# A graph layer kernel on one core: roots refined on GpSimd, half of the weights scaled on ScalarE, and another order of the front

## The reference

```python
h = relu(layernorm(x))                              # x: 2048 x 512, adj: 2048 x 2048, symmetric pattern
w_norm = (weight - mean(weight)) / std(weight, ddof=1)
wq  = round(clip(w_norm / wgt_alpha, -1, 1) * 7)    # weight: 512 x 512
xq  = round(min(h / act_alpha, 1) * 15)
support = relu((xq @ wq) * act_delta * wgt_delta)
sq  = round(min(support / act_alpha2, 1) * 15)
x   = x + ((adj / s) @ sq) * s * act_alpha2 / 15
h = relu(layernorm(x))
A = (adj + adj.T) / 2 + I;  d = rowsum(A) ** -0.5
x = x + adj @ ((d[:, None] * A * d[None, :]) @ h)
```

## Time and profile before

| | us |
|---|---|
| median of 3 runs (lowest, highest) | 508.2 (507.06, 508.78) |
| profiled execution | 508.43 |
| its span from first to last instruction | 506.5 |
| busy in it: PE | 489.6 (97%) |
| busy in it: DVE | 279.3 (55%) |
| busy in it: ACT | 141.3 (28%) |
| busy in it: POOL | 29.7 (6%) |

### The profile page before, as it was taken

The page is one execution under the profiler, slowest core; times in us unless marked ns, Lnnn a source line. Parts: engine busy times, 40 slices in busy tenths (PEclk is TensorE's granted clock), DMA queues, the critical chain, the costliest instruction groups (busy, mean ns, idle before and its releaser), DMA issues.

```text
span 506.5 us, 6411 instructions
## 1 busy us (share of the span) xinstructions
PE 489.6 (97%) x2404; PEld 238.8 (47%) x2404; DVE 279.3 (55%) x389; ACT 141.3 (28%) x198; POOL 29.7 (6%) x23
## 2 busy tenths in 40 slices
PE   2899999999899999999999999999999999999997
PEld 2646554554464444444444444444444444444443
DVE  5983989779979788787798777440010000100010
ACT  1576934425444143535431121240000000000000
POOL 0103710332000000000000000000000000000000
PEclk9999999999999999999999999999999999999999
DMA  8970676997944043232223322027001000000001
GB/s 295 402 299 1 177 155 164 212 257 167 291 139 146 0 128 122 83 118 89 83 84 124 122 85 83 0 79 274 21 22 41 21 21 21 34 28 21 21 21 41
DMA packets 39801, 56.86 MB, mean 112 GB/s; under 512 B 22888, under 2 KB 22888, under 8 KB 39784
## 3 DMA queue, kind: packets, MB, share of 16 engines
q1 hardware_dynamic: 39776, 56.63, 36.6%
q10 hardware_dynamic: 8, 0.00, 0.0%
HBM read 42.99 MB, written 8.39 MB: 101 GB/s over the span
## 4 chain that ended last, share of the span: by engine, by line
PE 90%; DVE 6%; DMA 2%; ACT 1%; issue 1%; ACTq 0%; POOL 0%; DVEq 0%; SPq 0%; POOLq 0%
PE ps_a L1020 33%; PE ps_p L919 18%; PE ps_p L983 7%; PE ps_a L983 7%; PE ps_b L983 7%; PE ps_m L983 4%; PE ps_h L983 4%; PE ps_a L901 2%; PE ps_b L901 2%; PE ps_b L873 1%; PE ps_m L919 1%; PE ps_h L919 1%; DVE st L552 1%; DVE small L774 1%; PE ps_a L873 1%; DMA a_in<-in_adj 1%
## 5 line engine op out<-in xcount | busy, mean ns | idle before, releaser
L919 PE MATMUL ps_p<-small,at 128*128 128x512 f16 x448 | 100.6, 379 | 0.0
L847 DVE SCALAR_TENSOR_TENSOR feat<-ps_a,feat 128x512 f32<-128x512 f32 x16 | 11.1, 691 | 153.8 <-PE ps_a L1020 153.8
L1020 PE MATMUL ps_a<-small,at 128*128 128x512 f16 x384 | 85.5, 379 | 0.0
L1020 PE MATMUL ps_a<-a_in,at 128*128 128x512 f16 x384 | 85.5, 379 | 0.0
L919 PEld LDWEIGHTS ps_p<-small,at 128*128 128x128 f16 x448 | 43.7, 98 | 47.9 <-DVE small L584 0.2
L457 ACT ACTIVATE split<-a_in 128x1024 f16<-128x1024 f32 x30 | 31.7, 1056 | 101.9 <-PE ps_p L983 90.0
L1020 PEld LDWEIGHTS ps_a<-a_in,at 128*128 (+1 forms) x384 | 37.6, 98 | 45.3
L1020 PEld LDWEIGHTS ps_a<-small,at 128*128 (+1 forms) x384 | 37.6, 98 | 45.3
L770 DVE TENSOR_TENSOR split<-a_in,split 128x1024 f16<-128x1024 f32 x30 | 36.7, 1224 | 34.0 <-ACT split L457 34.0
L983 PE MATMUL ps_p<-feat,split 128*128 (+1 forms) x180 | 43.9, 379 | 0.5 <-DVE small L774 0.5
L983 PE MATMUL ps_a<-feat,split 128*128 (+1 forms) x180 | 43.7, 379 | 0.0
(11 more groups left out here) (163 smaller groups left out, 422.6 us busy)
## 6 DMA issues: line engine op xcount, KB each, us to landing
a_in<-in_adj SPq DMA_DIRECT2D x54, 512.0 KB, 3.9
out<-feat SPq DMA_DIRECT2D x32, 256.0 KB, 2.4
feat<-in_x SPq DMA_DIRECT2D x8, 512.0 KB, 10.6
at<-in_adj SPq DMA_DIRECT2D x8, 512.0 KB, 14.2
feat<-out SPq DMA_DIRECT2D x4, 1024.0 KB, 9.5
at<-in_L_gnn_weight SPq DMA_DIRECT2D x2, 512.0 KB, 3.8
split<-in_adj SPq DMA_DIRECT2D x1, 512.0 KB, 16.5
tmp<-in_adj SPq DMA_DIRECT2D x1, 512.0 KB, 16.5
```

The lines of the kernel that those rows point to most:

```text
L847: nc.vector.scalar_tensor_tensor(xr, BANK[t % 2], 1.0 / (SA * SZ), xr, ALU.mult, ALU.add)\
L919: last = nc.tensor.matmul(l0_bank(r), at_block(r, lo, j), small[:, j * D:(j + 1) * D], start=(j == 0 and lo == 0), stop=(j == T - 1 and lo ...
L1020: last = nc.tensor.matmul(BANK[n], at_block(t, lo, j), z_part(j, z_lo), start=(j == 0 and lo + z_lo == 0), stop=(j == T - 1 and lo == 1))
```

## The change

- The factors `c_sup` and `c_out` are computed on GpSimd, behind the semaphore `factors`.
- The second half of the weights is scaled on ACT (`scale_weights_hi`) instead of DVE.
- Groups 1 to 4: DVE computes only the reciprocal of the root (`group_inverse`); GpSimd refines it by a step written in another form, inv x (0.75 − 0.25 x inv^2 x var), and forms the shift: one operation ahead, then five that each wait for the one before. Group 0 stays on DVE.
- `bn` and `aggr` signal and wait only where the aggregate reads the statistics, not after every instruction.
- The order of the front on ACT, DVE and PE is another one. `bn(0)` stands ahead of the weights' aggregate, `turn(1)` ahead of `transpose_rows(0)`, and the weights' factors right behind group 0.
- The 256-column memset on GpSimd is done early.

The new semaphores (`factors`, `factors_out`, `w_scaled1`, `root_inverse`, `pool_chain`) are declared beside the others. In the diff, "..." stands for lines of the old DVE order and for the declarations.

```diff
...
@@ -360,11 +365,40 @@
             pool.wait_ge(consts, 4)
             nc.gpsimd.tensor_copy(ident[:, :], ident32[:, :]).then_inc(consts, 1)
+            nc.gpsimd.memset(colp[:, :], 0.0).then_inc(zeroed, 1)
+            pool.wait_ge(factors, 1)
+            nc.gpsimd.tensor_scalar(c_sup, scal[:, 2:3], scal[:, 1:2], 1.0 / WGT_LEVELS, ALU.mult, ALU.mult)
+            nc.gpsimd.tensor_scalar(c_out, rec[:, 0:1], scal[:, 0:1], scal[:, 3:4], ALU.mult, ALU.mult).then_inc(factors_out, 1)
+            pool.wait_ge(factors_out, 1)
+            nc.gpsimd.tensor_scalar(c_sup, c_sup, rec[:, 3:4], None, ALU.mult)
+            nc.gpsimd.tensor_scalar(c_out, c_out, 1.0 / (ACT_LEVELS * SA), None, ALU.mult).then_inc(factors_out, 1)
             pool.wait_ge(c_wgt_ready, 1)
             nc.gpsimd.tensor_scalar(w_num[:, 0:2 * D].bitcast(i16), w_raw[:, 0:2 * D], c_wgt, b_wgt, ALU.mult, ALU.add)\
               .then_inc(w_scaled, 1)
-            nc.gpsimd.memset(colp[:, :], 0.0).then_inc(zeroed, 1)
+            links = [0]
+            def link(ins):
+                ins.then_inc(pool_chain, 1)
+                links[0] += 1
+                pool.wait_ge(pool_chain, links[0])
+            for n in range(1, len(GROUPS) - 1):
+                a, b = GROUPS[n], GROUPS[n + 1]
+                c = slice(a + 1, b + 1)
+                pool.wait_ge(var_ready, n + 1)
+                nc.gpsimd.tensor_scalar(shift[:, a:b], mv3[:, a:b, 0], -1.0, None, ALU.mult)
+                pool.wait_ge(root_inverse, n)
+                link(nc.gpsimd.tensor_tensor(nt2[:, c], inv[:, c], inv[:, c], ALU.mult))
+                link(nc.gpsimd.tensor_tensor(nt2[:, c], nt2[:, c], var[:, c], ALU.mult))
+                link(nc.gpsimd.tensor_scalar(nt2[:, c], nt2[:, c], -0.25, 0.75, ALU.mult, ALU.add))
+                link(nc.gpsimd.tensor_tensor(inv[:, c], inv[:, c], nt2[:, c], ALU.mult))
+                nc.gpsimd.tensor_tensor(shift[:, a:b], shift[:, a:b], inv[:, c], ALU.mult).then_inc(shift_ready, 1)
             for k, u in enumerate(ADDED):
                 pool.wait_ge(arr_sem(u), arrivals(u))
                 if k == 0:
@@ -426,8 +460,16 @@
                                                 ACT.Relu, bias=shift[:, t:t + 1], scale=inv[:, t + 1:t + 2])
                 last.then_inc(xn_ready, 1)
+            def scale_weights_hi():
+                act.wait_ge(c_wgt_ready, 1)
+                nc.scalar.activation(w_num[:, 2 * D:4 * D].bitcast(i16), w_raw[:, 2 * D:4 * D], ACT.Identity,
+                                     bias=b_wgt, scale=c_wgt).then_inc(w_scaled1, 1)
             def scale_support(m):
                 act.wait_ge(sup_ps, m + 1)
+                if m == 0:
+                    act.wait_ge(factors_out, 2)
                 if m >= 2:
                     act.wait_ge(sq_ready, m - 1)
                 nc.scalar.activation(sq[m % 2].bitcast(i16), sup_banks(m)[:, :], ACT.Relu, scale=c_sup)\
@@ -462,24 +504,25 @@
             group_root(0)
             normalise(0)
+            group_root(1)
+            scale_weights_hi()
             hi_turned(0)
...
-            hi_turned(1)
             group_root(2)
             normalise(1)
+            hi_turned(1)
             normalise(2)
             scale_support(0)
             normalise(3)
             group_root(3)
             scale_support(1)
+            scale_support(2)
             normalise(4)
-            scale_support(2)
+            group_root(4)
             normalise(5)
             scale_support(3)
...
             normalise(6)
+            normalise(7)
             scale_support(4)
-            normalise(7)
             scale_support(5)
             scale_support(6)
             scale_support(7)
@@ -546,15 +589,22 @@
             def stats(t):
                 return st[:, 24 + 6 * (t % 4):30 + 6 * (t % 4)]
+            seen = {}
             def bn(t):
                 if t % 2 == 0:
                     dve.wait_ge(x_in[t // 2], 16)
-                return nc.vector.bn_stats(stats(t), feat[:, t * D:(t + 1) * D])
-            def aggr(n, fill=None):
+                last = nc.vector.bn_stats(stats(t), feat[:, t * D:(t + 1) * D])
+                if t % 2:
+                    last.then_inc(chain, 1)
+                    count[0] += 1
+                    seen[t // 2] = count[0]
+            def aggr(n):
+                dve.wait_ge(chain, seen[n])
                 for t in (2 * n, 2 * n + 1):
                     last = nc.vector.bn_aggr(mv[:, 2 * t:2 * t + 2], stats(t))
-                link(last, fill)
+                link(last)
             def group_var(a, b):
                 nc.vector.tensor_scalar(var[:, a + 1:b + 1], mv3[:, a:b, 1], EPS, k_act, ALU.add, ALU.mult).then_inc(var_ready, 1)
@@ -584,14 +634,8 @@
                 nc.vector.tensor_scalar(small[:, 2 * m * D:2 * (m + 1) * D], sq[m % 2].bitcast(i16), float(ACT_LEVELS),
                                         None, ALU.min).then_inc(sq_ready, 1)
-            def scale_weights(h):
-                link(nc.vector.tensor_scalar(w_num[:, 2 * h * D:2 * (h + 1) * D].bitcast(i16),
-                                             w_raw[:, 2 * h * D:2 * (h + 1) * D], c_wgt, b_wgt, ALU.mult, ALU.add))
             def clamp_weights(h):
-                if h == 0:
-                    dve.wait_ge(w_scaled, 1)
+                dve.wait_ge(w_scaled1 if h else w_scaled, 1)
                 nc.vector.tensor_scalar(w_int[:, 2 * h * D:2 * (h + 1) * D],
                                         w_num[:, 2 * h * D:2 * (h + 1) * D].bitcast(i16),
                                         float(WGT_LEVELS), float(-WGT_LEVELS), ALU.min, ALU.max).then_inc(w_ready, 1)
@@ -621,80 +665,103 @@
                 link(nc.vector.tensor_scalar(scal[:, :], ps_m[:, 2:6], float(P), None, ALU.mult))
                 nc.vector.reciprocal(rec[:, :], scal[:, :])
                 nc.vector.tensor_scalar(k_act, scal[:, 2:3], scal[:, 2:3], 0.25 / ACT_LEVELS ** 2, ALU.mult, ALU.mult)
-                link(nc.vector.tensor_scalar(k_wgt, scal[:, 1:2], scal[:, 1:2], 0.25 / WGT_LEVELS ** 2, ALU.mult, ALU.mult))
-                nc.vector.tensor_scalar(c_sup, scal[:, 2:3], scal[:, 1:2], 1.0 / WGT_LEVELS, ALU.mult, ALU.mult)
-                link(nc.vector.tensor_scalar(c_out, rec[:, 0:1], scal[:, 0:1], scal[:, 3:4], ALU.mult, ALU.mult))
-                nc.vector.tensor_scalar(c_sup, c_sup, rec[:, 3:4], None, ALU.mult)
-                nc.vector.tensor_scalar(c_out, c_out, 1.0 / (ACT_LEVELS * SA), None, ALU.mult)
-            for k in range(KD):
+                nc.vector.tensor_scalar(k_wgt, scal[:, 1:2], scal[:, 1:2], 0.25 / WGT_LEVELS ** 2, ALU.mult, ALU.mult)\
+                  .then_inc(factors, 1)
+            def weight_stats(k):
                 if k % 2 == 0:
                     dve.wait_ge(w_in[k // 2], 16)
                 last = nc.vector.bn_stats(st[:, 6 * k:6 * k + 6], w_raw[:, k * D:(k + 1) * D])
-                if k == 1:
-                    scales()
-            link(last)
-            nc.vector.bn_aggr(wstat[:, 0:2], st[:, 0:6 * KD]).then_inc(wst_ready, 1)
+                if k == KD - 1:
+                    last.then_inc(chain, 1)
+                    count[0] += 1
+                    seen["w"] = count[0]
+            def weight_aggr():
+                dve.wait_ge(chain, seen["w"])
+                nc.vector.bn_aggr(wstat[:, 0:2], st[:, 0:6 * KD]).then_inc(wst_ready, 1)
+            def weight_spread():
+                dve.wait_ge(wst_ready, 1)
+                dve.wait_ge(wst_ps, 1)
+                link(nc.vector.tensor_tensor(wstat[:, 2:3], wstat[:, 0:1], ps_m[:, 0:1], ALU.subtract))
+                nc.vector.scalar_tensor_tensor(wstat[:, 3:4], wstat[:, 2:3], wstat[:, 2:3], wstat[:, 1:2],
+                                               ALU.mult, ALU.add).then_inc(wst_ready, 1)
+            def weight_var():
+                dve.wait_ge(factors, 1)
+                dve.wait_ge(wst_ps, 2)
+                nc.vector.tensor_scalar(var[:, 0:1], ps_m[:, 1:2], float(D * D) / float(D * D - 1), k_wgt,
+                                        ALU.mult, ALU.mult)
+            def weight_shift():
+                nc.vector.tensor_scalar(b_wgt, ps_m[:, 0:1], c_wgt, -1.0, ALU.mult, ALU.mult).then_inc(c_wgt_ready, 1)
+            def group_inverse(n):
+                a, b = GROUPS[n], GROUPS[n + 1]
+                dve.wait_ge(sd_ready, n + 1)
+                nc.vector.reciprocal(inv[:, a + 1:b + 1], nt1[:, a + 1:b + 1]).then_inc(root_inverse, 1)
+            weight_stats(0)
+            weight_stats(1)
+            weight_stats(2)
+            scales()
+            weight_stats(3)
             bn(0)
-            dve.wait_ge(wst_ready, 1)
-            dve.wait_ge(wst_ps, 1)
-            link(nc.vector.tensor_tensor(wstat[:, 2:3], wstat[:, 0:1], ps_m[:, 0:1], ALU.subtract))
-            nc.vector.scalar_tensor_tensor(wstat[:, 3:4], wstat[:, 2:3], wstat[:, 2:3], wstat[:, 1:2],
-                                           ALU.mult, ALU.add).then_inc(wst_ready, 1)
...
```

(142 more changed lines are left out.)

## The result

The changed kernel takes 505.38 us (median of 9 runs, 503.1 to 507.45), the kernel before 508.2 (median of 9, 506.81 to 511.0). The ratio is 0.9939, with a 95% interval of 0.9918 to 0.996: 2.8 us or 0.6% faster. The profiled execution took 505.38 with a span of 503.5, against 508.43 and 506.5.

A forecast was written before the change was run, and what follows sets the result against it. PE never waits from 26 us, so the gain is how much sooner `support(1)` starts: 1.0 us up to `support(0)` and 1.4 behind it, sum 2.5. 508.43 − 2.5 = 505.9, as a median 505.7; range 504.5 to 508.4.

The forecast's parts named there:

- Front up to the first root: Start of the kernel to group 0's root: gain nearly nothing, `normalise(0)` at 12.5 instead of 12.6 us.
- Term one: Front up to `support(0)`: it starts at 19.6 instead of 20.63, a gain of 1.0 us.
- The step sum from `bn(6)` on: DVE's operations from x landing at 14.9 to `clamp_rows(0)` ending at 19.55, just ahead of `support(0)`.
- Term two: From `support(0)` to `support(1)` at 23.35: PE's idle time falls from 2.55 to 1.1, a gain of 1.4 us.
- GpSimd's step: Refining operations of the roots on GpSimd: 0.33 us each, between bounds of 0.20 and 0.53.
- the hold beside DVE's clamps: Group 1's chain on GpSimd: 0.4 us added for waits beside DVE's two weight clamps, middle of 0 to 0.86.
- No stall behind `support(1)` up to 127 us: PE's waits behind `support(1)`, checked to `turn(3)`: slack of 0.3 to 1.3 us, so the order costs 0.
- PE's wait ahead of `support(0)`: PE idle some 2 us before `support(0)` at 19.6, longer than any gap since it sped up.
- rival d: PE's clock falls in the gap before 19.6, work to 26 takes some 3 us longer: 508.7; chance 0.06.
- step 3: DVE's work up to `support(0)`: it starts at 19.6, with PE's fourteen warming products done by 19.5.
- Rival a: At 130 us: PE's 1.44 us wait for adjacency rows takes back the whole 2.5, giving 508.2; chance 0.09.
- Rivals b and c: Front, GpSimd's small operations: at 0.45 to 0.65 us, gain 1.9 to −0.3 (chance 0.13); at 0.76 or more, slower (0.06).

The follow-up runs named there:

- E1: Changed kernel with the roots of groups 1 to 4 back on DVE: 507.43 us, ratio 0.9995 to the kernel before.
- E2: Changed kernel with the second half of the weights scaled on DVE again: 505.53 us, ratio 0.995 to the kernel before.
- E3: Changed kernel with the factors c_sup and c_out computed on DVE again: 505.07 us, ratio 0.9942 to the kernel before.
- E5: Changed kernel with an idle small operation ahead of each of GpSimd's five refining operations: 508.03 us, ratio 0.9983 to the kernel before.
- E8: Changed kernel without the warming products that only keep PE busy: 507.5 us, ratio 0.9984 to the kernel before.
- E4: Changed kernel with roots, second half of the weights and factors all back on DVE, only order and fewer waits kept: 510.73 us, ratio 1.0033.
- E10: Kernel before the change, with GpSimd's last addition made to wait for DVE's low part of unit 23: 507.73 us, ratio 0.9986.

## Why the prediction was right

505.7 was predicted, a gain of 2.5; 505.38 was measured, a gain of 2.8.

- Front up to the first root, nearly nothing: right, by a slightly wrong sum. `bn(0)` waits 0.46 for x, and the root of group 0 is even 0.07 sooner than before (11.30 and 11.37). But `bn(3)`, now ahead of `group_scale(0)`, holds DVE to 11.78 and not to 11.5, so that `group_scale(0)` starts at 11.78, 0.2 later than before instead of 0.1 earlier. The wait for x at `bn(4)` took it up.
- Term one, `support(0)` at 19.6: measured 19.75, a gain of 0.9 instead of 1.0. The step sum from `bn(6)` on was right to 0.15, and E1 and E2 show its terms (1.63 for the four small steps that each of two groups leaves, 0.2 a step; 0.86 for the weights).
- Term two, `support(1)` at 23.35: measured 23.06, a gain of 1.9 behind `support(0)` instead of 1.4. GpSimd's step was 0.28 instead of 0.33, and the hold beside DVE's clamps 0.27 (1.61 − 1.34) instead of 0.4; the shift of group 1 was ready at 18.05, not 18.25.
- The Trainium skill, "SBUF — State Buffer", section "Who interferes with whom", had the clamps of weights, with one SBUF input and in a two-port mode, hold GpSimd. The trace agrees: 0.29 and 0.39 for operations of 0.20, each ending with the clamp; which mode the clamp ran in, no trace shows. In the same section the Trainium skill has two SBUF inputs on DVE contend with a GpSimd operation that reads SBUF. The operations near 118 us show it in both directions: DVE's took 2.33 instead of 1.19 in the changed kernel, GpSimd's 3.29 instead of 2.35 in E3.
- No stall behind `support(1)` up to 127 us: right.
- PE's wait ahead of `support(0)`: I wrote some 2 us in rival d, though step 3 of my own sum had the warming products end at 19.5. It was 0.78, since fourteen products are 28 matmuls and took 3.34. I gave the clock's fall 0.06. The mechanism is real; in E5, E8 and E4 it cost 1.5, 1.9 and 2.3 us up to the instruction behind `support(1)`. My evidence for it, a granted clock of 1.00 beside the slow first turns, was from the earlier trace rows, which begin at 26 us; the busy table of 10 to 13 us reads 1.00 too, in both kernels.
- Rival a, that the stall takes the gain back, did not happen, and it moves with PE. The wait that I named for it was wrong: the row sum at 123.82 does not release the load. In E10 ACT's row sum runs from 123.92 and the load is issued at 123.62. The load stands in SP's queue behind the transpose of unit 23's low part, which waits for DVE. I took the stall's 1.4 as there in every run, apart from the hold that "may take the 1.4 away". It is there or not by which of two instructions is first.
- Rivals b and c, GpSimd too slow: the sum they went by is right (E5: `support(1)` 1.98 later, 2 by the sum), the step was not reached.

## What to carry to other kernels

Price an instruction taken off an engine by whether a wait stands between it and the next mark: the roots' small steps were worth 1.6 us behind the last arrival of x, the factors' nothing ahead of it. Read a median together with the clock of its runs: two kernels can differ by how often their clock falls, and a profile shows one execution only. When a front is shortened or reordered, the products that only keep PE busy have to be fitted again, since too many stand in the way and too few let the clock fall. Where two engines hold each other, fix the order of the two instructions by a semaphore if one of them feeds a load that PE waits for.

## What the runs showed of the hardware

- A GpSimd operation of the refining step on 128 x 2 or 128 x 4 f32 took 0.20 us, and a dependent one started 0.28 after it; DVE's step is 0.20.
- With PE idle for 3.65 (E4) or 5.04 us (E8) the granted clock went to 0.50, and with gaps of 1.02, 1.86 and 0.47 around one support set and two transpose sets too (E5). Gaps of 0.78 and 0.47 (changed) and of 1.44 and 0.41 (E2) left it at 1.00. The slow pace of the first turns (1.97 for eight transposes) stands beside a granted clock of 1.00 in the table.
- A two-input addition on GpSimd (2.35 by itself) and a two-input operation on DVE (1.19), all in SBUF, never ran at once where they met near 118 us: whichever was second took up to 3.4.
